# VectorE's corner product in front of the attention moved behind LayerNorm, third place and logits

## What is computed

```python
# layer 0
xp = x @ w_in + b_in
h = gelu(batch_norm(depthwise_conv_3x3(x)))
offset = (h @ w_off + b_off).reshape(N, H, W, GROUP, P, 2)
mask = softmax((h @ w_msk + b_msk).reshape(N, H, W, GROUP, P))
samp = bilinear_sample(pad(xp), places(offset))      # four corners of each tap
y = einsum('nghwpc,nhwgp->nhwgc', samp, mask) @ w_out + b_out
x = x + gamma1 * layer_norm(y, ln1_g, ln1_b)
m = gelu(x @ w_fc1 + b_fc1) @ w_fc2 + b_fc2
x = x + gamma2 * layer_norm(m, ln2_g, ln2_b)
# layer 1
t = x.reshape(N, H * W, C)
t = t + causal_attention(_ln_t(t), Wq, Wk, Wv)
t = t + top2_of_8_experts(_ln_t(t), router_w, expert_w)
```

## Time and profile before

| | |
|---|---|
| median of three runs | 14408.87 us (14386.05 to 14408.93) |
| profiled execution, its own time | 14354.76 us |
| profiled execution, span | 14352.9 us |
| TensorE busy | 7279.6 us, 51% |
| VectorE busy | 5255.5 us, 37% |
| ScalarE busy | 3605.8 us, 25% |
| GpSimd busy | 6152.5 us, 43% |
| granted TensorE clock, mean | 0.717 |

### The profile page before, as it was taken

The page is one execution under the profiler, slowest core; times in us unless marked ns, Lnnn a source line. Parts: engine busy times, 40 slices in busy tenths (PEclk is TensorE's granted clock), DMA queues, the critical chain, the costliest instruction groups (busy, mean ns, idle before and its releaser), DMA issues.

```text
span 14352.9 us, 82620 instructions
## 1 busy us (share of the span) xinstructions
PE 7279.6 (51%) x24978; PEld 4003.5 (28%) x24978; DVE 5255.5 (37%) x11405; ACT 3605.8 (25%) x6964; POOL 6152.5 (43%) x6507
## 2 busy tenths in 40 slices
PE   3445555454554555445554545644555455544456
PEld 2222222222322322223232223322222222222223
DVE  2333343433434333333434334333434333333334
ACT  2222222222222222222222212222222222222232
POOL 5454443445344444444434453344444444344530
PEclk6667777776776777777776767767777677776677
DMA  3111111111111111111111111111111111111110
GB/s 69 39 44 42 36 42 35 43 37 43 37 38 44 39 41 37 40 43 38 44 33 42 38 44 41 32 45 39 40 39 37 45 38 40 31 35 36 41 30 11
DMA packets 670424, 562.89 MB, mean 39 GB/s; under 512 B 389530, under 2 KB 565890, under 8 KB 670032
## 3 DMA queue, kind: packets, MB, share of 16 engines
q0 software_dynamic: 208656, 426.82, 10.7%
q1 hardware_dynamic: 460704, 130.97, 4.1%
q10 hardware_dynamic: 672, 0.24, 0.0%
HBM read 487.56 MB, written 69.97 MB: 39 GB/s over the span
## 4 chain that ended last, share of the span: by engine, by line
another core or an unknown queue 41%; PE 20%; DVE 18%; issue 11%; ACT 9%; SPq 0%; DMA 0%; DVEq 0%; ACTq 0%
DVE ring L1080 4%; PE bank L1518 4%; DVE y L1092 4%; ACT arena L809 4%; PE bank L1637 3%; PE bank L1651 3%; ACT arena L812 3%; PE bank L1613 1%; PE bank L1718 1%; PE bank L1794 1%; PE bank L1773 1%; DVE y L1096 1%; PE bank L1574 1%; ACT pT L873 1%
## 5 line engine op out<-in xcount | busy, mean ns | idle before, releaser
L723 POOL DMA_INDIRECT ring<-column_table,idx_r x6468 | 6128.5, 948 | 7904.9 <-DMA wts_r<-corner_weight 5889.8
L1518 PE MATMUL bank<-arena,stripes 116*128 116x448 f32 (+1 forms) x3360 | 1628.5, 615 | 1108.7 <-ACT arena L812 649.5
L1092 DVE TENSOR_REDUCE y<-ring 128x96 f32<-128x3456 f32 x196 | 1188.4, 6063 | 17.9 <-DVE ring L1080 7.2
L1518 PEld LDWEIGHTS bank<-arena,stripes 116*128 116x128 f32 (+1 forms) x3360 | 662.7, 213 | 1868.0 <-issue 1071.1
L1651 PE MATMUL bank<-pT,xh 112*128 112x448 f32 (+3 forms) x1792 | 876.5, 574 | 560.3 <-ACT pT L873 327.3
L1154 DVE TENSOR_TENSOR z<-bank,b_fc 128x512 f32<-128x512 f32 (+1 forms) x56 | 35.0, 624 | 2874.6 <-remote 2806.7
L1637 PE MATMUL bank<-qT,kT 128*112 128x448 f32 (+3 forms) x1792 | 856.9, 567 | 366.3 <-ACT qT L867 229.5
L1176 DVE TENSOR_TENSOR part<-bank,part 128x448 f32<-128x448 f32 x168 | 104.5, 622 | 2458.8 <-PE bank L1518 1397.7
L1080 DVE TENSOR_TENSOR ring<-ring,bank 128x4224 f32<-128x4224 f32 x196 | 892.1, 4551 | 18.7 <-DVE part L1176 11.9
L812 ACT ACTIVATE arena<-arena,dcol 116x896 f32<-116x896 f32 x840 | 875.1, 1042 | 27.4
L1496 PE MATMUL bank<-ident,drow 112*116 112x112 f32 x1344 | 275.4, 304 | 1075.2 <-issue 1001.2
(11 more groups left out here) (192 smaller groups left out, 8934.4 us busy)
## 6 DMA issues: line engine op xcount, KB each, us to landing
ring<-column_table,idx_r POOLq DMA_INDIRECT x6468
column_table<-proj SPq DMA_DIRECT2D x196, 112.0 KB
corner_weight<-wts_s SPq DMA_DIRECT2D x56, 252.0 KB
wts_r<-corner_weight SPq DMA_DIRECT2D x196, 72.0 KB
tin<-tokens SPq DMA_DIRECT2D x56, 224.0 KB
out<-xn SPq DMA_DIRECT2D x56, 224.0 KB
xin<-in_x SPq DMA_DIRECT2D x49, 224.0 KB
x<-in_x SPq DMA_DIRECT2D x28, 256.0 KB
```

The source lines that it names most:

```text
L723: pool.indirect_dma_start(ring[:, r, e * CORNERS:(e + 1) * CORNERS, :].rearrange("p s c -> p (s c)"), None, source, bass.IndirectOffsetOnA ...
L1092: step.did(dve.tensor_reduce(y[:, k % BLK % 2, 0:(G - 1) * CG].rearrange("p (g c) -> p g c", c=CG), terms[:, 0:whole].rearrange("p (g e) c ...
L1518: pe.matmul(bank[SUM_BANKS[d]][:, 0:CH], stripes[0:rows, k, :], hats2[item % HAT_PAIRS][0:rows, k % 2 * CH:(k % 2 + 1) * CH], start=(k == ...
```

## The change

The product of the half slot's first tile leaves the head of VectorE's `attention`. It stands directly in front of that tile's sum, since `tile` is `multiply` and then `sum_up`. No instruction is added or removed, and no other engine's program is touched.

```diff
@@ attention, VectorE
                 g = i * NJ + j
                 buf = 1 - h
                 u0 = units(i, j, 0)
-                if first:
-
-                    multiply(*first)
                 if now:
                     for d in range(DENSE - 1):
                         set_place(dense_chunk(*now)[2], d, h)
@@
                     p, f = ahead
                     read_logits(2 * p + f // NJ, f % NJ)
                 if first:
-                    sum_up(*first)
+                    tile(*first)
                 for q in range(NT):
                     for c in range(j + 1):
                         m = q * (j + 1) + c
```

## The result

The changed kernel takes 14638.9 us, median of 4 runs (14624.96 to 14646.25). The kernel before, on the same chip, takes 14397.46 us, median of 4 (14380.54 to 14408.93). The ratio is 1.0164, 95% interval 1.015 to 1.0178: slower by 236 us (216 to 256). The forecast of 195 us more is 41 us short and lies outside that interval. The spans of the two profiled executions are 14644.4 - 14352.9 = 291.5 us apart: the one of before (14354.76 us) was 43 us under its median, the one of after (14646.25) 7 us over.

A forecast was written before the change was run, and what follows sets the result against it. No engine bound the kernel; VectorE's stretch from MLP's end to the maxima was taken to be on the path. 208 - 15 + 2 = 195 us, added to the median of the runs, gave 14604 us, range 14500 to 14695.

The forecast's parts named there:

- the main mechanism: VectorE from MLP's end to maxima: on the path; product stops covering LayerNorm's load and costs 4.80 us ahead of the sum.
- Most signs named ahead: LayerNorm waits 2 to 3 us for `tin` in over 50 half slots; sum 4 to 5 us later; weights copy waits.
- The rigid shift: Likeliest case: everything behind the late sum moves along with it; 14604 us, range 14540 to 14665, chance 78%.
- One sign of being wrong: Long stalls at L1154 or L1239 get shorter; the other was later score waits shrinking by as much as the sum is late.
- The loss at the sum: Sum in 47 half slots with a front: 26 x 4.80 = 125 us, plus 83 us in 21 others, together 208 us.
- There nothing is won at all: Third place where it already waits over 0.2 us, 26 half slots: no gain upstream, full 4.80 us lost each, 125 us.
- the `yT` copy: ScalarE, behind its first hat's wait for the first place: copy and L1496 come a little sooner; part of some 4 us.
- ScalarE and the maxima: Hats slide with the sum; 11 us back in the maxima's wait, some 4 us from two other things: 15 us off.
- the clock rival: TensorE's longer gap before the first hat halves its clock: up to 2.31 x 47 = 108 us more, 14712, chance 12%.
- The half slots without a front: Six half slots: sum 2.6 us late, three or four end level or 1 us ahead, two lose 2.6; +2 us together.
- LayerNorm did start 1.46 us sooner: Rival at LayerNorm: its start 1.5 us sooner in 53 half slots decides, 80 us faster, 14329 us; chance 4%.
- The gathers didn't swallow the shift: Rival at VectorE's stalls under gathers: the shift falls into them and costs nothing, 14409 to 14440 us; chance 6%.

The follow-up runs named there:

- the kept-busy kernel: The changed kernel plus seven matmuls into a bank nobody reads, between the first and second hat's matmuls: 14543.59 us, ratio 1.015 to the kernel before.

## Why the prediction was right, and where its sizes were off

**The direction and the main mechanism held.** VectorE's stretch from the MLP's end to the maxima is on the path; the product gave up a cover (the trip of `tokens` to `tin`) and paid its full time in front of the sum. Most signs named ahead came: 51 more waits for `tin`, MLP's end to LayerNorm down to 5.63 us in the median (about 5 was said), 0.25 us idle ahead of the sum, the weights copy waiting about 5 us (4.86) for the product, GpSimd's idle time growing by the loss. The sum's delay, said to be 4 to 5 us, is 3.8 in the median. The rigid shift was the likeliest case and the time lies in its own range.

**One sign of being wrong came too.** The prediction was to be wrong if the long stalls at L1154 or L1239 got shorter. L1154's unseen waits did, from 2806.7 to 2467.8 us; L1239's wait for TensorE didn't (1327.1 and 1370.7). The sign was badly chosen: with the first two places ahead of the product L1154 waits 3066.2 us, 260 more than before, and the time is the same. The long stalls move between instructions from kernel to kernel. What L1154 lost turned up at the maxima (229 us more), at `keep_z` L1068 (157 more) and at L1417, the old L1420 (127 more).

**The loss at the sum: 208 us forecast, 164 found** (47 x 3.49). The step that failed is "There nothing is won at all: TensorE's front doesn't depend on the product, and the loss is the full 4.80", for the 26 half slots whose third place had waited. Fifteen of them are undisturbed, and they lose 3.05 us in the mean, fewer than the 15 others (3.94); 26 x 3.05 is 79 us and not 125. The other 21 half slots were sized well, 3.97 forecast and 3.94 found. In the fifteen, L1496's end comes 1.80 us sooner behind the MLP's end in the mean (median 1.57). A part of that hangs on what stands behind the product: its first `project` waits for VectorE's two places through ScalarE's hat and the `yT` copy, which comes 1.18 us sooner in the median where the end of the front's own matmuls (L1718, now L1715) comes 0.58 us sooner. I had seen the `yT` copy, and booked it at 4 us for the whole program. The rest is there already at the end of those matmuls (1.44 us sooner in the mean), and nothing here ties it to the product; the fifteen were also picked by a long wait before, and in three of them it was simply shorter this time (sums 0.10 to 1.08 us late). How the loss that didn't come divides between the two stays open.

That doesn't hold for every half slot. In the one shown above, TensorE finished L1715 6.75 us behind the MLP's end, where it was 5.85 before (2826.14 + 7.64 - 2827.93). The third place won 0.26 us instead of the 1.13 worked out, and the sum is 4.55 late.

**ScalarE and the maxima: 15 us back forecast, 65 us more found.** "The hats slide with the sum and cost little of their own" is right for ScalarE: L777 stands 0.15 us ahead of the sum in the median, where it was 0.32. It is wrong for TensorE. Its first three scores end 2.45 us before the sum starts in the median, where they ended 2.35 us after that. It multiplies the first hat and then stands still for 5.5 us (0.5 before); then come the other hats near half clock, the last four 2.53 us instead of 1.73 in the mean. This is the clock rival, which I put at up to 2.31 us per half slot and gave 12%. My reason against it, that VectorE has three maxima to read first, hides part of it: what's left is 1.39 us, 65 us in all if none of it is swallowed later, as an addition to the shift and not in its place.

**The half slots without a front: +2 us forecast.** Sums 2.4 to 2.9 us late where 2.6 was worked out, and the fourth maximum 1.2 and 0.3 us sooner and 0.9 and 3.0 us later in the four that no long stall touches. That sums to the forecast. In the other two a long stall falls ahead of the fourth maximum, and it can't be read there.

**Rivals.** LayerNorm did start 1.46 us sooner in the mean of the undisturbed half slots (1.5 forecast), and where there is a front that decided nothing: the fourth score waits for the hats there. The gathers didn't swallow the shift on this chip. With a pause of over 5 us taken as the end of a burst, the time inside the gathers' bursts is 8072 us before and 8093 after, outside them 6281 and 6552.

**The balance.** 164 + 65 + 2 = 231 us, against 236 measured and 195 forecast. The two errors had opposite signs, -44 and +80, so that the forecast was closer than its parts is luck. The balance is no proof either: the same sum misses the product behind LayerNorm by 55 us (134 against 79) and the kept-busy kernel by 40 (175 against 215). What was shown is the price of each of three places, the load's trip behind LayerNorm's wait, and the clock behind the late fourth score. What the last 78 us are made of was only argued.

## What to carry to other kernels

A product that covers a trip through DRAM costs most of its duration where it is moved to (here 3.5 of 4.80 us), since little is won where it stood; before moving it, look for what it hides where it stands, and not only for what it delays where it goes. If an engine's work is moved so that TensorE gets a pause of several us, price the matmuls behind the pause at half clock (here 0.75 us instead of 0.42 after 5.8 us of standing still), and check whether someone waits for them: with the product behind the third place they were slow too and nobody did. And when an operation that releases other engines (here the weights copy and with it the hats) is moved, follow the release as well as the operation.

## What the runs showed of the hardware

The kernel before took 14.34 to 14.41 ms on two chips and 8.41 to 8.42 ms on two others; the change 14.64 and 8.40 ms. GpSimd's gathers are as fast on both (L723 949 and 950 ns each). What differs is what other engines do under them. A burst of gathers of the kernel before on the first kind of chip and the stretch behind it, then a burst of the change on the second kind. Columns: stretch, us, busy time of PE, PEld, DVE, ACT, POOL with counts, granted clock, DMA share, GB/s.

```profile
7273.05:7355.40 82.35, 20.31 (x95) 13.83 (x94) 17.48 (x25) 5.62 (x13) 62.55 (x66) 0.60 0.19 56
7360.00:7395.00 35.00, 25.40 (x85) 13.50 (x86) 30.08 (x71) 16.01 (x25) 0.00 (x0) 0.84 0.18 41
```

```profile
1634.00:1675.00 41.00, 37.31 (x123) 18.44 (x122) 26.06 (x49) 22.90 (x38) 31.25 (x33) 1.00 0.23 63
```

In these stretches TensorE works 20 of 82 us on the first kind while gathers run, and 37 of 41 on the second. How it looks from inside, in the kernel before: VectorE's Newton steps (the reciprocal root of a LayerNorm) come 1.40 us apart although each needs only the one before it, and TensorE's matmuls L1496 come singly, 2.80 us apart. GpSimd gathers in both stretches.

```profile
7102.96 0.16 DVE L992 SCALAR_TENSOR_TENSOR nwt<-nwt 128x4 f32<-128x4 f32 x1 [1.24 <-DVE nwt L990]
7104.36 0.17 DVE L988 TENSOR_TENSOR nwt<-nwt 128x4 f32<-128x4 f32 x1 [1.24 <-DVE nwt L992]
7105.77 0.17 DVE L990 TENSOR_TENSOR nwt<-nwt 128x4 f32<-128x4 f32 x1 [1.24 <-DVE nwt L988]
```

Such steps of the changed kernel (of 112 rows instead of 128) with no gathers about, 0.20 us apart:

```profile
12970.30 0.17 DVE L988 TENSOR_TENSOR nwt<-nwt 112x4 f32<-112x4 f32 x1
12970.50 0.17 DVE L990 TENSOR_TENSOR nwt<-nwt 112x4 f32<-112x4 f32 x1
```

And TensorE's matmuls of the kernel before:

```profile
7309.64 0.26 PE L1496 MATMUL bank<-ident,drow 112*116 112x112 f32 x1 [2.54 <-issue]
7312.44 0.35 PE L1496 MATMUL bank<-ident,drow 112*116 112x112 f32 x1 [2.54 <-issue]
```

Those are the long stalls whose releaser the profile doesn't see. The gathers of the tiles take 8052 us in all in the changed kernel on the first kind and 8059 on the second, and the pauses between one tile's gathers and the next's 6253 and 59 us: nearly all of the time that separates these two executions lies in the pauses (6194 of 6240 us). Why one kind of chip does this was not found. It decides whether a change to the parts between the gathers counts: the change costs 1.64% on one kind (1.015 to 1.0178) and nothing that can be told from noise on the other (0.9984 to 1.0002).
